# The first unit's logits moved from the stage of slots to the end of the stage of norms

## The reference: an attention layer, then a soft mixture of experts

```
x  = LN(x + attention(x))                         # 16 heads, 4 groups, causal
xl = LN(x) * gamma + beta                         # [b, n, 512]
logits   = einsum(xn, mu_n)                       # xn: xl at unit length; mu_n: 16 experts x 128 slots
dispatch = softmax(logits over tokens)
slot_in  = einsum(xl, dispatch)                   # per batch and expert: [128 slots, 512]
slot_out = gelu(slot_in @ W1 + b1) @ W2 + b2
out      = einsum(slot_out, softmax(logits over all slots))
x  = LN(x + out)
```

## Time and profile before

| what | value |
|---|---|
| median of three runs | 2499.29 us |
| profiled execution, whole | 2497.7 us |
| its span in the trace | 2496.0 us |
| PE busy | 2400.8 us, 96% of the span |
| mean granted TensorE clock | 0.979 of full |
| DVE, ACT, POOL busy | 1735.2, 1426.8, 1610.6 us |

### The profile page before, as it was taken

How to read it: one execution, slowest core, us unless ns; L and a number is a source line. 1 busy time by engine, 2 the same in 40 slices (tenths; PEclk the granted TensorE clock), 3 DMA queues, 4 the chain that set the end, 5 groups by cost and what they waited for, 6 DMA issues and landing times. The chain is left out here.

```text
span 2496.0 us, 38932 instructions
## 1 busy us (share of the span) xinstructions
PE 2400.8 (96%) x12834; PEld 1717.9 (69%) x12834; DVE 1735.2 (70%) x3804; ACT 1426.8 (57%) x2761; POOL 1610.6 (65%) x1751
## 2 busy tenths in 40 slices
PE   8999999999999999998979999998999997999998
PEld 6875455555555555545757888876888885888886
DVE  3378888888888888726875566576565654777776
ACT  3225566666666666664865555566565654454543
POOL 4405678687776777787956666765766675455553
PEclk9999999999999999999989999999999997999999
DMA  7863657475656666556964454567544447664553
GB/s 250 270 193 88 138 120 150 101 151 116 138 124 144 127 134 129 106 115 227 338 185 144 132 166 139 159 192 197 160 142 153 150 146 247 212 210 130 149 153 102
DMA packets 249177, 400.87 MB, mean 161 GB/s; under 512 B 57712, under 2 KB 112016, under 8 KB 237584
## 3 DMA queue, kind: packets, MB, share of 16 engines
q1 hardware_dynamic: 195864, 283.46, 37.2%
q0 software_dynamic: 52480, 114.37, 20.6%
q10 hardware_dynamic: 632, 0.56, 0.1%
HBM read 180.63 MB, written 112.22 MB: 117 GB/s over the span
## 5 line engine op out<-in xcount | busy, mean ns | idle before, releaser
L1155 ACT ACTIVATE p_probs<-p_ps_s 128x512 f32<-128x512 f32 (+3 forms) x1280 | 591.4, 540 | 319.1 <-PE p_ps_s L1073 308.4
L1741 POOL DMA_DIRECT2D p_eT<-p_ex x1024 | 538.4, 535 | 273.6 <-DVE p_ex L2007 222.2
L1182 DVE TENSOR_REDUCE p_parts<-p_ps_m 128x1 f32<-128x512 f32 x752 | 458.4, 680 | 73.7 <-PE p_ps_m L1058 73.4
L1073 PE MATMUL p_ps_s<-q,k_e 98*128 98x512 f32 (+3 forms) x1280 | 467.0, 387 | 3.9 <-ACT p_probs L1155 3.5
L995 POOL TENSOR_TENSOR p_added<-p_added,p_probs 128x2048 f32<-128x2048 f32 x88 | 420.0, 4782 | 30.9 <-ACT p_probs L1155 17.0
L1058 PE MATMUL p_ps_m<-k_m,q 96*128 96x512 f32 (+3 forms) x1232 | 431.1, 384 | 6.6 <-PEq L2282 3.9
L1073 PEld LDWEIGHTS p_ps_s<-q,k_e 98*128 98x128 f32 x1280 | 240.3, 191 | 181.5 <-issue 77.7
L1058 PEld LDWEIGHTS p_ps_m<-k_m,q 96*128 96x128 f32 x1232 | 231.6, 191 | 84.9 <-DVE p_parts L1188 22.3
L1091 PE MATMUL p_ps_c<-p_probs,v_e 128*32 128x512 f32 (+3 forms) x2560 | 283.4, 543 | 5.1 <-POOL p_probs L975 5.0
L2141 POOL TENSOR_TENSOR p_acc<-p_acc,logit 128x512 f32<-128x512 f32 x112 | 162.4, 1450 | 153.3 <-ACT logit L2194 149.8
L1188 DVE CUSTOM_DVE_ANT_0 p_masked<-p_ps_m,p_mask 128x128 f32<-128x128 f32 (+1 forms) x480 | 203.6, 485 | 25.0 <-PE p_ps_m L1058 24.9
(11 more groups left out here) (204 smaller groups left out, 4975.6 us busy)
## 6 DMA issues: line engine op xcount, KB each, us to landing
p_probs<-p_probs POOLq DMA_DIRECT2D x56, 1024.0 KB, 7.5
logits_t<-logit SPq DMA_DIRECT2D x32, 1024.0 KB, 5.0
p_eT<-p_ex POOLq DMA_DIRECT2D x1024, 32.0 KB, 2.0
logit<-logits_t SPq DMA_DIRECT2D x128, 256.0 KB, 3.4
q<-q_t SPq DMA_DIRECT2D x96, 256.0 KB, 4.7
c_first<-L_ffn_W_dram SPq DMA_DIRECT2D x64, 256.0 KB, 5.6
p_probs<-p_probs POOLq DMA_DIRECT2D x16, 768.0 KB, 7.4
p_x<-L_attn_x_dram SPq DMA_DIRECT2D x32, 256.0 KB, 4.8
```

Of the source, the lines that this page charges most:

```text
L1073: pe.matmul(ps_s[:, u % ST_BANKS, q0:BLK], k_e[:, bass.ts(kt, P)], q[:, qb, h, q0:BLK], start=True, stop=True).then_inc(s_score, 1)
L1155: act.activation(probs[s % RING][:, h, q0:BLK], ps_s[:, u % ST_BANKS, q0:BLK], ACT.Exp).then_inc(s_exp, 1)
L1182: dve.tensor_reduce(to, bank, AX.X, ALU.max).then_inc(s_taken, 1)
L1741: pool.dma_start(eT[r][p * QD:(p + 1) * QD, i, :, :], ex[i * QD:(i + 1) * QD, 2 * r:2 * r + 2, bass.ts(p, P)]).then_inc(s_eT[r], 16)
```

## The change

The four banks into which norms projects become shared with the logits' banks of slots (`banks`). Unit 0's logits are computed at the end of norms: `first_logits(0)` to `(2)` stand on PE's queue behind the transposes of tiles 27, 28 and 29, and `first_logits(3)` behind the last transpose. For that the slot vectors are fetched at i == 16 in place of 32 and split at step 32 (ACT `vectors_hi`, DVE `vectors_lo`); expert 1's are fetched and split at the end of the stage too. In slots, PE begins with the logits of unit 1 and ACT with the copies of unit 0. The second half of unit 0's moves is issued by SP (`first_moves`), behind the rows and the store of the logits. The splits of the rows' second half go from the end of step 1 to their places in step 2.

```diff
--- before.py
+++ after.py
-def post(nc, sems, x, bo, gamma, beta, scale, mu, b1_t, d, kept, ready, s_ctx_st, stored):
+def unit_vectors(ready):
+    quarter = lambda k: ready[1][:, k, :].rearrange("p (c s) -> p c s", c=DC)
+    return [quarter(r) for r in range(2)], [quarter(2 + r) for r in range(2)]
+
+def post(nc, sems, x, bo, gamma, beta, scale, mu, b1_t, d, kept, ready, s_ctx_st, stored, banks):
...
-        ps_p, ps_t = al.psum("p3_ps_p", R4), al.psum("p3_ps_t", R4)
+        ps_p, ps_t = banks, al.psum("p3_ps_t", R4)
... post, sync
             for i in range(TT + 8):
-                if i == TT:
+                if i == TT // 2:
                     fetch_kept()
+                if i == TT + 1:
+                    sp.wait_ge(s_mlo, 1)
+                    sp.dma_start(kept_mu[:, :, :], mu_e[:, 1, :, :]).then_inc(s_mu, 16)
... post, tensor
+            def first_logits(j):
+                if j == 0:
+                    pe.wait_ge(s_mlo, 1)
+                pe.wait_ge(s_y, TT - JG + j + 1)
+                pe.wait_ge(s_xtlo, (j + 1) * TG)
+                for c in range(DC):
+                    part = bass.ts(c, P)
+                    mm = three_passes(pe, ps_p[:, j, :], m_hi[0][:, c, :], m_lo[0][:, c, :],
+                                      kept_hi[:, j * TG:(j + 1) * TG, part], kept_xT[:, j * TG:(j + 1) * TG, part], c == 0, c == DC - 1)
+                mm.then_inc(s_first, 1)
+
             for i in range(TT + 8):
                 if i < TT:
                     project(i)
                 if 0 <= i - 5 < TT:
                     transpose(i - 5)
+                if TT <= i < TT + JG - 1:
+                    first_logits(i - TT)
+            first_logits(JG - 1)
... post, scalar
+            def vectors_hi(n):
+                act.activation(m_hi[n][:, :, :], kept_mu[:, :, :], ACT.Copy).then_inc(s_mhi, 1)
+
             for i in range(TT + 8):
+                if i == TT:
+                    act.wait_ge(s_kept, 48)
+                    act.wait_ge(s_proj, TT)
+                    vectors_hi(0)
...
+            act.wait_ge(s_mu, 16)
+            vectors_hi(1)
... post, vector
+            def vectors_lo(n):
+                dve.wait_ge(s_mhi, n + 1)
+                dve.tensor_tensor(m_lo[n][:, :, :], kept_mu[:, :, :], m_hi[n][:, :, :], ALU.subtract).then_inc(s_mlo, 1)
+
                 if 0 <= i - 1 < TT:
                     centred(i - 1)
+                if i == TT:
+                    vectors_lo(0)
...
+            vectors_lo(1)
... slots
-        ps_l, ps_s, ps_e = al.psum("p4_ps_l", JG), al.psum("p4_ps_s", 1), al.psum("p4_ps_e", 1)
+        ps_l, ps_s, ps_e = banks, al.psum("p4_ps_s", 1), al.psum("p4_ps_e", 1)
+        logits_to = lambda count: count - JG
+        def moved(n, r):
+            if r == 0:
+                return s_eT[r], 256 * (n + 1)
+            return (s_eT[r], 256 * n) if n > 0 else (s_eT_first, 256)
... slots, sync
             def load_mu(n):
-                if n > 0:
-                    sp.wait_ge(s_mulo, n)
+                if n >= 2:
+                    if n > 2:
+                        sp.wait_ge(s_mulo, n - 2)
                     sp.dma_start(m_raw[:, :, :], mu_e[:, n % E, :, :]).then_inc(s_mu, 16)
+            def first_moves(n):
+                if n == 0:
+                    sp.wait_ge(s_turn, 4)
+                    for p in range(NQ):
+                        for i in range(NQ):
+                            sp.dma_start(eT[1][p * QD:(p + 1) * QD, i, :, :],
+                                         ex[i * QD:(i + 1) * QD, 2:4, bass.ts(p, P)]).then_inc(s_eT_first, 16)
-                 + [(1, first_rows), (1, store_logits)] + [(2, load_weights)] + ...
+                 + [(1, first_rows), (1, store_logits), (1, first_moves)] + [(2, load_weights)] + ...
... slots, gpsimd
-                for r in range(2):
+                for r in range(1 if n == 0 else 2):
... slots, tensor
-            pe.wait_ge(s_id, 1)
             def logits(j):
                 def part(n):
                     r = n % 2
-                    if j == 0:
-                        pe.wait_ge(s_mulo, n + 1)
+                    if n == 0:
+                        return
+                    if j == 0 and n >= 2:
+                        pe.wait_ge(s_mulo, n - 1)
... slots, scalar (the vector queue's rows_lo likewise)
             def rows_hi(j, first):
                 def part(n):
-                    if starts(n) and (n == 0) == first:
+                    if starts(n) and (n == 0 and j < JG // 2) == first:
             def copy(j):
                 def part(n):
-                    act.wait_ge(s_log, 4 * n + j + 1)
                     if n > 0:
+                        act.wait_ge(s_log, logits_to(4 * n + j + 1))
                         act.wait_ge(s_most, 4 * n - JG + j + 1)
                         act.wait_ge(s_ex, 4 * n - JG + j + 1)
                         act.wait_ge(o_l, 16 * n)
-                 + [(1, rows_hi(j, True)) for j in range(JG)] + [(2, weights_hi), (2, largest_row)])
+                 + [(1, rows_hi(j, True)) for j in range(JG // 2)] + [(2, weights_hi), (2, largest_row)])
```

More of the change, by code:

```diff
@@ L1564, in _, with slots @@
                     variance(i)
-JG = 4
+            vectors_lo(1)
 STAGE = 4
-TG = NT // JG
 QD = 32
 NQ = P // QD
-def slots(nc, sems, mu, W1, W2, b2, d, kept, more, ready, stored, handed):
+def slots(nc, sems, mu, W1, W2, b2, d, kept, more, ready, stored, handed, banks):
     with ExitStack() as ctx:
@@ L1586, in slots @@
         quarter = lambda e, k: e[:, k, :].rearrange("p (c s) -> p c s", c=DC)
[L1587 removed]
+        m_lo, m_hi = unit_vectors(ready)
         eT_lo, eT_hi = ([quarter(ready[0], 2 * half + r) for r in range(2)] for half in range(2))
```

49 lines of the change are left out of this document (31 added, 18 removed).

## The result

The changed kernel takes 2512.40 us (median of five runs, 2512.03 to 2515.58), where the kernel before, beside it, takes 2500.62 (2498.82 to 2501.35). The ratio on record is 1.004, with a 95% interval from 1.0027 to 1.0053: slower, as forecast, by more. (The ratios on record are not the quotients of the two medians printed beside them, which here would be 1.0047; by the ratio the change costs 10.0 us, by the medians 11.8.) It was measured again in the experiments: 2511.57 against 2500.92, ratio 1.0046 [1.0033, 1.0058]. The forecast was 2506.6, and its range ended at 2511, so the median lies 1.4 us above the range; the ratio, taken of the 2499.29 us on which the forecast was built, gives 2509.3, inside it.

A forecast was written before the change was run, and what follows sets the result against it. PE, busy for 96% of the span, bounds the kernel. Landing 1310.4 + 18.5 = 1328.9 against 1321.6, 7.3 us later; 2497.7 + 7.3 = 2505.0, with 1.6 for the median 2506.6 us, range 2497.5 to 2511.

The forecast's parts named there:

- Norms: End of norms: `first_logits(0)` from 1264.65, `first_logits(3)` from 1279.5 for 2.8 us; slots begin at 1283.4, 10.1 us later.
- Unit 1's logits: Start of slots: they wait only for unit 0's `copy(0)` and run 1284.2 to 1295.3; 7 us gained up to here.
- The landing of the store: SP's queue in slots: unit 0's logits land behind the rows at 1310.4 (1307 to 1313); the products wait for it.
- The 2 us, and the 4 at the other end: Slots' transfer line: POOL's sixteen moves beside the rows lengthen it by 2 us, taken between 4 us and nothing.
- From the landing to the mark: Slots: `product(0)` at L + 3.3, `product(2)` L + 11.5, `product(3)` L + 15.7, ending L + 18.5; later splits cost 1.5 us.
- the mark: First logits of unit 2 on PE, at 1321.62 before; forecast at 1328.9, 7.3 us later.
- L: In slots, the time when the store of unit 0's logits lands: 1310.4, range 1307 to 1313.
- The step that failed: Behind unit 2's first logits the work is the same in the same order, so the end shifts equally, 7.3 us.
- the second half of moves: SP's moves behind rows and store in slots: land some 2 us behind L, wanted at L + 7.6; worth nothing here.
- A: Same chain, shorter: moves take nothing from the rows (L 1308.4); 3 to 5 us later, about 2503 us; chance 0.28.
- B: Store not held behind the rows, lands 4.6 us after issue; POOL's first half last; 4.5 us earlier, 2495 us; chance 0.13.
- C: SP's moves land behind L + 8, cut into smaller pieces, holding `product(2)`: 2 to 4 us more, 2510 us; chance 0.05.

The follow-up runs named there:

- the last two experiments: Three quarters of the rows loaded in norms, all splits early, against the changed kernel: with SP's moves 2501.85 us, with all moves by POOL 2499.86 us.

## Why the prediction was right, and what it left out

The direction and the wait that decides were right; the size was 7.3 us, where 10.0 to 11.8 were measured. Each step, by before's clock (4.33 taken off).

**Norms.** `first_logits(0)` was forecast at 1264.65, after a wait of 4.25 from 1260.4. It came at 1264.69, after 4.22, at clock 0.50. The two below were right as well, and the last transposes ended at 1277.6. `first_logits(3)` began at 1279.45, forecast 1279.5. It was to take 2.8 us at full clock, but the granted clock fell to 1.2 GHz again after the wait of 1.9 us, and it took 4.5. Slots began at 1284.95, forecast 1283.4. This is the first term that was too small, by 1.5 us in this trace.

**Unit 1's logits** ended by 1296.9, forecast 1295.3, later by that same 1.5. They were 5 us ahead of before's, and nothing came of it.

**The landing of the store.** Forecast 1310.4, measured 1310.6 (ACT's copy at 1315.07 less 4.33 is 1310.7). The sum was right because two terms erred against each other: the line began 1.5 us late, and it was 25.3 us long from the first row's issue (1289.63) to the landing (1315.0), not 26.6. Beside 24.6 in before, it is 0.7 us longer with POOL's sixteen moves under way, where I had taken 2; and even that is near the spread, for the other three traces of before's layout have 25.1, 24.7 and 23.5, the second of the changed kernel 25.1, and the one in which POOL issues all 32 moves 25.4.

The 2 us, and the 4 at the other end, came from the earlier trace rows, a reading that charged the moves with too much. On SP's queue a store of logits and the weights stood just ahead of the other batch's rows, so the 8 us were not the price of the moves alone:

```profile
1684.58 0.32 SPq L1685 DMA_DIRECT2D logits_t<-logit  x1
1684.94 0.67 SPq L1691 DMA_DIRECT2D c_first<-L_ffn_W_dram  x1
1685.66 1.39 SPq L1692 DMA_DIRECT2D c_first<-L_ffn_W_dram  x1
...
1687.64 9.82 SPq L1663 DMA_DIRECT2D xl_lo<-x_ln  x16
```

The Trainium skill's rule on turns between queues ("DMA: Bandwidth & Descriptors", "Queues, rings and completion order"), priced by the earlier trace rows, would have put the landing at 1312.4. The turns are there: from 1300.0 to 1311.0 in the changed kernel's trace the packets of POOL's queue (0.5 MB) stand among those of SP's, which moved 237 GB/s before (1291 to 1299) and 194 beside them (1301 to 1309). The size was not borne out. The page's other rule, that descriptors on one ring are consumed in order, agrees with the traces: 14.5 us for the store behind the rows, 8.0 on ACT's queue.

**From the landing to the mark.** `product(0)` at L + 3.4 (forecast 3.3), `product(2)` at L + 11.6 (11.5), `product(3)` at L + 15.8 (15.7), the mark at L + 18.7 (18.5). The late splits cost 2.4 us, as the kernel with early ones shows, and not 1.5 (2.3 to 2.5 by the two traces of the changed kernel).

**The sum.** The mark moved by 7.7 us from one trace to the other, forecast 7.3. Over the traces that share a layout, norms take 10.4 us more (mean of six, 143.4, against mean of four, 133.0) and slots 4.2 less (44.3 in two, against 48.4 in two), which is 6.2.

**The step that failed** is the sentence that the shift of the mark is the shift of the end, since what lies behind is the same work in the same order. It isn't quite: the stage's end costs 1.6 to 1.8 us more with SP's moves. I had costed the second half of moves at nothing, and it is nothing only up to the mark. At the stage's end POOL comes last, and not SP: its closing instruction takes 10.5 us where it took 2.7 (last section). The kernel before with that part alone shows the price by itself, and two pairs of kernels that differ in that part alone (the changed one and its like with POOL's moves, and the last two experiments) show it going away. In the list of costs this is a term of 1.7 us that was missing.

6.2 to 7.7 and 1.7 make 8 to 9.4 us. Measured are 10.7 and 11.8 by the medians, 10.0 and 11.5 by the ratios. The rest, 1 to 4 us, stays open. In the means of the same six and four traces the stages ahead of norms take 1.4 us more, the work from the mark to DVE's last instruction of slots 1.3 us more, and output 0.2 us more; with these the sum is 10.8. But the four traces of before's layout differ among themselves by 5.7 us in the first piece and by 3.0 in the second, so whether the change costs anything there is not shown.

**The rivals.** A (a shorter line, 2503) was right on the moves, which took little, and wrong on the start of slots, which was later and not earlier. B (the store isn't held behind the rows) is out for this kernel. It holds in the kernel where ACT issues the store, and there the gain that B promised (4.5 us faster than before) doesn't come: slots get 4.2 us shorter than in the changed kernel, the time stays 5.8 us above before's, and POOL's moves are last then. B had them land 2 us behind POOL's last issue, and it was 6.0 (1304.1 to 1310.1). C (SP's moves late) didn't come to pass; ACT split the third tile at 1323.4 without waiting for a landing.

## What to carry to other kernels

When a stage's boundary moves later, everything that starts with the stage moves with it. Moving 13.6 us of matmuls across the boundary had PE done with the next unit's logits 5 us sooner, but the line of transfers behind the boundary began 10 us later and became the bound, so ask first which chain starts at the boundary, and move its head too. With three quarters of the rows loaded before the boundary, the splits early and the moves back on POOL, the same idea turned from 0.4% slower to 0.2% faster.

Cost a transfer by its place on its queue: the same store landed in 14.5, 8.9 or 8.0 us by what stood ahead of it. And compare the far ends of stages as well as the place of the change: a part that looked free gave back 1.7 us eight hundred microseconds later, where another engine closed the stage.

## What the runs showed that was not expected

SP issuing sixteen 32 KB moves near the start of slots goes with a longer passage from slots to output, 2.8 to 4.6 us of idle time on DVE in nine traces, against 1.84 to 1.87 in five without. The trace tells which engine it is. Each engine closes the stage with a DRAIN, an instruction that the rows of the timelines leave out (POOL's and SP's stand at L1619 in the changed kernel), and output begins about 1.3 us (1.26 to 1.33) behind the end of the later of the two in all fourteen traces. POOL's DRAIN takes 2.7 us where POOL issues all moves and 10.5 us where SP issues sixteen of them. Three pairs of kernels that differ in that part alone:

| kernel | POOL's DRAIN, us | it ends | SP's ends | output begins |
|---|---|---|---|---|
| before | 2.68 | 2109.44 | 2112.94 | 2114.22 |
| SP's moves alone | 10.51 | 2119.23 | 2117.45 | 2120.55 |
| both halves by POOL | 2.67 | 2121.78 | 2126.02 | 2127.31 |
| changed | 10.52 | 2127.32 | 2125.72 | 2128.63 |
| three quarters, POOL's moves | 2.68 | 2112.48 | 2115.74 | 2117.01 |
| three quarters, SP's moves | 10.51 | 2118.23 | 2115.44 | 2119.53 |

So the cost is what POOL's DRAIN reaches beyond SP's, 0.9 to 2.8 us. Why it takes 10.5 us and not 2.7, with sixteen of POOL's 1024 moves gone, isn't shown.

In the changed kernel the granted clock fell to half at 1284.9, 1.1 us into `first_logits(3)`, behind an idle time of 1.9 us; PE had been at full clock from 1274.6 to then. The second trace of the same kernel has no such fall: its `first_logits(3)` takes 3.0 us and not 4.5. It gained little by that, 0.5 us in norms, since its `first_logits(0)` had begun 2.3 us later (125.5 us after norms' first projection, against 123.2). Of the ten traces with logits in norms eight have the fall there and two have not.
